# Graph layer on one core: GpSimd's first additions ahead of the reciprocal root, ScalarE's sum copy between two halves of normalising, the b3 seed and VectorE's output sum later

## What is computed

```python
agg_edge = jax.ops.segment_sum(edge_attr, dst, num_segments=12500)   # 12500 x 48
hn = jnp.maximum(_layernorm(x), 0.0)                                 # 12500 x 128
c = jnp.concatenate([hn, agg_edge], axis=1)                          # 12500 x 176
h = jax.nn.silu(c @ W1 + b1)                                         # 256 wide
h = jax.nn.silu(h @ W2 + b2)                                         # 256 wide
out = x + hn + (h @ W3 + b3)                                         # 12500 x 128
```

## Time and profile before

| | us |
|---|---|
| median of 3 runs | 308.7 (308.48 to 309.76) |
| the profiled execution | 308.38 |
| its span (first to last instruction) | 306.5 |

### The profile page before, as it was taken

How to read it: one execution, slowest core, us unless ns; L and a number is a source line. 1 busy time by engine, 2 the same in 40 slices (tenths; PEclk the granted TensorE clock), 3 DMA queues, 4 the chain that set the end, 5 groups by cost and what they waited for, 6 DMA issues and landing times.

```text
span 306.5 us, 12286 instructions
## 1 busy us (share of the span) xinstructions
PE 287.6 (94%) x4378; PEld 256.4 (84%) x4379; DVE 245.6 (80%) x620; ACT 224.8 (73%) x435; POOL 121.6 (40%) x240
## 2 busy tenths in 40 slices
PE   6973969999999999999999999999999999999994
PEld 5763849998899889988899888988899888999993
DVE  7788877798887988888888978888888988875560
ACT  8773667778767877778677877779777887779762
POOL 3055534343544345332443435333553435434200
PEclk9996979999999999999999999999999999999999
DMA  5998347556866578555864577555885568731111
GB/s 162 311 289 227 85 129 208 148 155 188 245 180 164 147 233 240 162 140 177 240 194 142 162 220 240 147 151 182 239 228 157 155 192 238 211 95 35 32 31 57
DMA packets 79218, 53.15 MB, mean 173 GB/s; under 512 B 2928, under 2 KB 78794, under 8 KB 79184
## 3 DMA queue, kind: packets, MB, share of 16 engines
q1 hardware_dynamic: 79184, 52.70, 59.8%
HBM read 46.29 MB, written 6.40 MB: 172 GB/s over the span
## 4 chain that ended last, share of the span: by engine, by line
PE 46%; issue 21%; POOL 16%; DVE 8%; POOLq 5%; ACT 1%; DVEq 1%; ACTq 0%
POOL agg_carry L450 12%; PE z L1089 10%; PE agg_ps L1020 10%; POOL rstd L425 4%; PE z L1073 4%; PE z L1077 4%; PE z L1074 4%; POOLq L430 3%; PE z L1053 3%; PE z L1058 2%; PE z L1055 2%; PE z L1059 2%; PE z L1054 2%; PE stage L1024 2%; PE tp L1037 2%
## 5 line engine op out<-in xcount | busy, mean ns | idle before, releaser
L450 POOL TENSOR_TENSOR agg_carry<-staged,agg_carry 48x42 f32 x195 | 80.3, 412 | 79.5 <-POOL agg_carry L450 30.1
L1020 PEld LDWEIGHTS agg_ps<-onehot,raw 128*48 128x48 f32 x1568 | 73.2, 125 | 11.4 <-issue 11.3
L708 DVE TENSOR_TENSOR onehot<-window,rel 128x1176 f32<-128x1176 f32 (+1 forms) x57 | 77.2, 1355 | 5.8 <-DVE stats L683 4.1
L1020 PE MATMUL agg_ps<-onehot,raw 128*48 128x42 f32 x1568 | 77.2, 214 | 1.9 <-DVE onehot L708 1.6
L1024 PE MATMUL stage<-onehot,raw 128*48 128x42 f32 x1560 | 76.9, 214 | 0.0
L425 POOL TENSOR_TENSOR rstd<-vareps,minus_half 112x4 f32<-112x4 f32 (+1 forms) x28 | 38.6, 1377 | 89.2 <-DVE vareps L693 89.2
L1024 PEld LDWEIGHTS stage<-onehot,raw 128*48 128x48 f32 x1560 | 72.8, 125 | 0.1
L1089 PE MATMUL z<-w,h 128*112 128x128 f32 (+1 forms) x448 | 56.1, 278 | 0.8 <-ACT h L563 0.8
L1089 PEld LDWEIGHTS z<-w,h 128*112 128x112 f32 (+1 forms) x448 | 50.5, 176 | 2.4 <-ACT z L555 1.1
L534 ACT ACTIVATE xn<-x_t,nmr,rstd 112x128 f32<-112x128 f32 (+1 forms) x112 | 45.8, 479 | 2.2 <-DVE nmr L701 2.2
L542 ACT ACTIVATE hT_hi<-tp 128x448 fp32r<-128x448 f32 (+1 forms) x28 | 15.2, 544 | 42.7 <-PE tp L1037 42.6
(11 more groups left out here) (119 smaller groups left out, 435.8 us busy)
## 6 DMA issues: line engine op xcount, KB each, us to landing
raw<-in_edge_attr_dram SPq DMA_DIRECT2D x55, 672.0 KB, 5.5
x_t<-in_x_dram SPq DMA_DIRECT2D x27, 224.0 KB, 6.2
out_dram<-out_t SPq DMA_DIRECT2D x27, 224.0 KB, 5.8
dst_rows<-in_dst_dram SPq DMA_DIRECT2D x1, 512.0 KB
raw<-in_edge_attr_dram SPq DMA_DIRECT2D x1, 288.0 KB, 3.5
dst_rows<-in_dst_dram SPq DMA_DIRECT2D x1, 256.0 KB, 2.8
out_t<-in_L_gnn_W_dram SPq DMA_DIRECT2D x1, 256.0 KB, 7.4
x_t<-in_x_dram SPq DMA_DIRECT2D x1, 192.0 KB
```

The source lines that it names most:

```text
L450: pool.tensor_tensor(into, staged[:, parity, k // 2, :], into, ALU.add).then_inc(s_odd, 1)
L708: return dve.tensor_tensor(onehot[:, slot, at * PER:n * PER, :], window[:, :].unsqueeze(1).broadcast_to([P, cols_n, WINDOW]), cols.unsquee ...
L1020: mm = pe.matmul(banks[0:ED, bass.ds(offsets[(k - first) // 2], WINDOW)], edges, into, start=False, stop=True, skip_group_check=True, tile ...
```

## The change

Four moves, and no instruction is added but the ones for the wait of the second half of normalising.

- GpSimd: in a step the three early additions of batch i+1 stand ahead of `rstd_of(i+1)`, and the four late ones behind it. Before, `rstd_of` was ahead of all seven.
- ScalarE: `stage_sums` stands between quarters 0, 1 and quarters 2, 3 of `normalize`, not behind all four.
- ScalarE: `seed_b3` stands behind `activate1`, ahead of `normalize`, not between the two Silu of `activate2`. `clear_bank` takes its place there.
- VectorE: `finish` stands behind `relu_lo` and `agg_lo`, not ahead of them.

```diff
@@ gpsimd step
                 if has(i, -1, NB):
                     nodes = nodes_of(i + 1)
+                    add_odd(i + 1, 1 - parity, nodes, True)
                 if has(i, -1, NT):
                     rstd_of(i + 1, 1 - parity)
                 if has(i, -1, NB):
-                    add_odd(i + 1, 1 - parity, nodes, True)
                     add_odd(i + 1, 1 - parity, nodes, False)
@@ scalar normalize, activate2
-            def normalize(i, turn):
+            def normalize(i, turn, quarters=range(PER)):
...
-                for q in range(PER):
+                for q in quarters:
                     ln = act.activation(xn[0:np_, parity, q, :], x_t[0:np_, turn, q, :], ACT.Identity,
                                         bias=nmr[0:np_, parity, q:q + 1], scale=rstd[0:np_, parity, q:q + 1])
-                ln.then_inc(s_xn, 1)
+                if q == PER - 1:
+                    ln.then_inc(s_xn, 1)
...
-            def activate2(t):
+            def activate2(t, m):
                 n = PER * nodes_p(t)
-                for m in range(M):
-                    act.wait_ge(s_z2, M * t + m + 1)
-                    wait(act, s_z3, t)
-                    act.activation(h2[:, m, 0:n], z[:, m, 0:n], ACT.Silu,
-                                   bias=b2c[:, m:m + 1]).then_inc(s_h2, 1)
-                    if m == 0:
-                        seed_b3(t)
+                act.wait_ge(s_z2, M * t + m + 1)
+                wait(act, s_z3, t)
+                act.activation(h2[:, m, 0:n], z[:, m, 0:n], ACT.Silu,
+                               bias=b2c[:, m:m + 1]).then_inc(s_h2, 1)
@@ scalar step
                 if has(i, 2, NT):
-                    activate2(i - 2)
+                    activate2(i - 2, 0)
                 if has(i, 1, NT - 2):
                     act.wait_ge(s_carried, i)
                     clear_bank(1 - parity)
+                if has(i, 2, NT):
+                    activate2(i - 2, 1)
                 if has(i, 1, NT):
                     activate1(i - 1)
-                if has(i, 0, NT) and not (isinstance(i, int) and i == NT - 1):
-                    normalize(i, turn)
+                if has(i, 2, NT):
+                    seed_b3(i - 2)
+                now = has(i, 0, NT) and not (isinstance(i, int) and i == NT - 1)
+                if now:
+                    normalize(i, turn, range(0, PER // 2))
                 if has(i, -1, NB):
                     stage_sums(i + 1, 1 - parity)
+                if now:
+                    normalize(i, turn, range(PER // 2, PER))
@@ vector step
                 if has(i, 1, NT):
                     carry_over(i - 1, 1 - parity)
+                    relu_lo(i - 1)
+                    agg_lo(i - 1)
                 if has(i, 3, NT):
                     finish(i - 3, 1 - parity)
-                if has(i, 1, NT):
-                    relu_lo(i - 1)
-                    agg_lo(i - 1)
```

## The result

| kernel | median us | lowest to highest | the profiled execution | its span |
|---|---|---|---|---|
| before, in the same session | 309.23 | 308.48 to 310.54 | 308.38 | 306.5 |
| after | 317.94 | 316.11 to 319.15 | 316.11 | 314.2 |

The ratio is 1.028, with a 95% interval of 1.024 to 1.033: the change makes the kernel slower. The forecast was 309.5 with a range up to 311.7, so the result lies outside it. The two profiled executions differ by 7.7 us in their spans. (The medians differ by 8.7: the profiled execution after is the fastest of its four, so about 1 us of the loss is in no trace.) Where the 7.7 us sit is read from starts in both timelines (`agg` is L853 before and L858 after, layer 1 L1053 and L1057). Tiles are counted from 0.

A forecast was written before the change was run, and what follows sets the result against it. The prediction took a 9.66 us ring of VectorE and GpSimd to set the pace. Its terms, −2.8 (start) − 0.04 (kept slack) + 3.6 (end) = +0.8, gave a median of 309.5 us, range 307.2 to 311.7.

The forecast's parts named there:

- The exclusion of addition and building: Loop: GpSimd's first addition waits for VectorE's building with two SBUF operands, so moving it ahead of `rstd` gains 0 us.
- The seeds' three waits: Last three steps: layer 3 waits for its b3 seed, 1.15, 2.0 and 0.5 us, sum 3.6.
- Layer 1's other wait: Loop: layer 1 also waits for `h2` part 0, going on 0.15 after its end, so only 0.04 us is gained.
- The cover of the transposes: Loop: normalising, done later, still ends 0.4 us before the transposes follow layer 3's matmuls; cost 0.
- The times of the start up to layer 1 of tile 1: Start: `agg` at 38.55, 1.0 us sooner; transposes 1.4 later; TensorE idle about 0.4 before layer 1, which comes 1.0 sooner.
- The end.* Here b3 loses its cover: Steps 27 to 29: layer 3 waits for the later b3 seed with nothing to hide it, +3.6 us.
- VectorE's own total is unchanged, thus its ring too.: Loop: moving the output sum behind `hT_lo` and `agg_lo` leaves VectorE's 9.66 us ring as it was.
- The rival with late additions: Loop: late additions delay `agg_lo`, 0.1 us in some 23 steps, 2.4 us, giving 311.9; chance 0.16.
- the start: Start: earlier `agg` and no half clock, with effects in the two next steps, gain 2.8 us, or 1.6 if the clock falls.
- Its two terms with rows, 1.0 and 1.55: Start: `agg` of tile 1 comes 1.0 us sooner; 3.1 us at half clock, costing 1.55, is taken as gone.
- The terms at zero: Loop: early additions, later `rstd`, later b3 seed and later normalising were each costed at 0 us per step.
- VectorE's ring: Loop: closed ring of VectorE and GpSimd, `agg` to building to additions to next `agg`, 9.66 us, sets the pace.

The follow-up runs named there:

- h_winps: Kernel before with `window` in PSUM instead of SBUF: 301.73 us, ratio 0.974.
- a_seed: Kernel before with only the b3 seed moved behind `activate1` and `clear_bank` in its place: 314.04 us, ratio 1.018.
- f_resid4: Kernel after with four buffers for `resid` instead of two: 314.37 us, ratio 1.015.
- j_end: Kernel after with four `resid` buffers, the last tile's `rstd` first, and seeds and output sums of the last three steps placed as before: 307.48 us, ratio 0.997.
- g_best: Kernel after with four `resid` buffers, `rstd` first in step 26 and seeds between the Silus in the last three steps: 309.94 us, ratio 1.003.
- l_afterwin: Kernel after, whole change, with `window` in PSUM: 314.90 us, ratio 1.018 against the kernel before.
- a_split: Kernel before with only the `staged` copy moved between the halves of `normalize`: 308.80 us, ratio 1.000.
- e_start: Kernel before with the early additions ahead of `rstd` in step 1 only: 307.50 us, ratio 0.995.
- a_pool: Kernel before with only the three early additions moved ahead of `rstd`: 310.79 us, ratio 1.007.
- m_winsplit: Kernel before with `window` in PSUM and the `staged` copy between the halves of `normalize`: 308.18 us, ratio 0.999 against the kernel before.

## Why the prediction was wrong

**What held.** The exclusion of addition and building: nothing changed in the loop when `rstd` left its place, and h_winps shows the cause directly. The rule of the Trainium skill on which it leaned (page "SBUF — State Buffer", section "Who interferes with whom") agrees: with two SBUF operands in the building the addition waits for its end in every step, with one it does not. The seeds' three waits, 3.6 forecast and 3.70 measured. Layer 1's other wait, 0.14 behind the Silu. The cover of the transposes, 0.45 us for 0.4. The times of the start up to layer 1 of tile 1.

**First wrong step: the end.** "*The end.* Here b3 loses its cover" looked only at the seeds. The forecast did follow `rstd` past the additions, but in a plain step, where its reader comes 1.9 us after `agg` starts. In step 26 the last tile's `nmr` is in front of `agg`, and its `rstd` stands behind additions that wait for the copy of `staged`. Missed: +2.17, so the end costs 5.87 and not 3.6. Also missed was that the clock falls behind these gaps in some executions (3.66 and 3.55 us for a layer 3 of 2.00, in a_seed and f_resid4).

**Second: "VectorE's own total is unchanged, thus its ring too."** It was, but a move also changes distances between instructions of one engine. `add_x` waits for a semaphore that `finish` gives; with `hT_lo` and `agg_hilo` in between that was free, with only `nmr` in between it costs 0.11 us in every step, 2.55 us in all. The rival with late additions had the right size (0.1 per step, 2.4 us) and the right engine for the wrong reason: `agg_hilo` stays at 0.62, and with four buffers the loss is gone while the additions are where they were.

**Third: the start was mis-sized.** −2.8 was forecast, −1.42 came. (Its two terms with rows, 1.0 and 1.55, sum to 2.55; no run shows the rest.) `agg` of tile 1 comes 0.96 sooner. From there to `agg` of tile 2 it is 10.31 us before, 9.85 after, and 8.95 in j_end, whose order is the same there but which has no stop of TensorE. So the clock gives 1.36, and the stop takes 0.90 back (−0.96 − 1.36 + 0.90 = −1.42).

What the stop waits for is not settled. It comes in ten of the sixteen traces, h_winps among them, where nothing is reordered. In each of the ten SyncE's two loads of edges, issued in the same stretch, are recorded over 2.3 to 2.8 us (2.56 in the kernel after, from 44.37), and in the six without it over 1.5 to 1.7. g_best has both the stop and the long issue, and j_end, with the same order up to step 26, neither. (l_afterwin has no stop there, but one of 0.78 us at 53.63, and there too an issue of 2.46 us, from 52.62.) So the stop isn't the additions'; what holds the two engines up is open.

The clock's part wasn't tied to the additions either. In a_seed and a_split, with the additions unchanged, the granted clock stays at 1.00 too (TensorE is idle for 2.06 and 0.97 us before layer 1 instead of 2.75), and layer 1 of tile 2 comes 24.11 and 24.27 us after the first `agg`. In the kernel after it is 24.14, in the kernel before 25.54. So in these traces the clock alone is worth the whole start, and the stop takes back what the additions gain. That e_start is 0.5% faster shows that its edit gains something, not which of the two gives it.

**The terms at zero.** Of the other moves that were costed at nothing in the loop, the split costs 6.4 us and the seed 3.5 us where VectorE's ring doesn't hide them (`window` in PSUM). Here it hides them. The forecast was right to name the cover, and should have kept the price without it in the range: the sum was made of small differences between large terms of both signs.

**Left over** are the 0.70 us at tile 25. Layer 3 of the step before has a stop without a releaser there: 0.32 us in the kernel after (at 274.50), 0.25 to 0.94 in eight of the other kernels that keep `window` in SBUF, and none before or in j_end. It is not the split's alone, since a_pool (0.67), e_start (0.39) and a_seed (0.25) have it. Its cause is open.

In all: forecast −2.8 − 0.04 + 3.6 = +0.8; measured −1.42 + 2.55 + 0.70 + 5.87 = +7.7.

## What to carry to other kernels

Follow a moved instruction through the steps that are written out, each by itself: the first and the last steps have other neighbours, and one wait there cost as much as 20 steps of the loop. Look for waits of an engine on its own semaphore before bringing producer and consumer closer together; the list of waits did not show one of 0.11 us, and more buffers removed it. When a wait is explained by an exclusion, try to remove the exclusion rather than what stands beside it: one operand in PSUM gave 2.6%, the whole reordering with its costs mended nothing that can be told from noise.

## What the runs showed of the hardware

- A VectorE comparison of 128 × 1176 takes 1.38 us with both operands in SBUF and with one in PSUM, but only in the first case does a GpSimd addition (0.25 us by itself) wait for its end.
- `resid`, which waits for the semaphore of VectorE's own `out_t` just ahead of it, starts 0.11 us after that record's end. An instruction without such a wait starts about 0.08 before the end of the record ahead of it.
- TensorE can stop for up to 1.2 us with nothing in the profile to wait for. In layer 2 its matmuls did so only in the kernels where `xn` is whole 0.45 us ahead of the transposes (10 times in m_winsplit), and not in those with 0.97 or 1.49 us.
- In ten traces TensorE stopped for 0.6 to 1.2 us in the edge sums between 43 and 48 us, while SyncE's issue of two loads was recorded over 2.3 to 2.8 us; in the six others it ran through there, and the issue took 1.5 to 1.7. It is seen, not explained.
- At the start, 2.75 us of idle TensorE were followed by half the clock for 3.1 us in the kernel before, and 2.06 us in a_seed by none of it. At the end, gaps of 1.8 us were followed by half the clock in two kernels' executions (a layer 3 of 3.66 and 3.55 us) and by none of it in the kernel after (2.00).
